# Slots of an expert-routed layer dealt four side by side to a partition, the slot table read in 4 KB rows, and early tile 5 turned ahead of the wait for that table

## The chip, the cores and the metric

The kernel runs on one core of one Trainium2 chip. TensorE (PE) multiplies; VectorE (DVE), ScalarE (ACT) and GpSimd (POOL) do the elementwise work; SyncE (SP) issues transfers; 16 DMA engines move the data. The time is device microseconds (us) of one launch. The median of three runs of the kernel before is 891.31 us, from 889.29 to 902.32.

## What is computed

```
y      = einsum('bct,bcd->bdt', x, cond_weights[itok])   # x: 64 x 64 x 1024 f32
logits = y @ W_gate + b_gate                             # 8 experts
top    = top_k(logits, 2)
out    = x + mean over the two chosen experts of relu(y @ W_e + b_e)
```

There are 64·64 = 4096 tokens of 1024 features. Each goes to two of eight experts, whose matrices are 1024 x 1024 in f32.

## The kernel before

**Token stage.** For 32 tiles of 128 tokens (n = 0 to 31) PE makes y (line 549), ACT copies it out (701) and writes it to `y_rows` in DRAM (704), and DVE turns it in 32 x 32 blocks (856) for the gate product (561). Every four tiles form a group g. For it DVE picks the top two experts (`choose`, 879) and works out each token's place in its expert's list (`slots`, 894). PE and DVE make the lists (`fill`, `list_out`), and SP writes them to `slot_table` in DRAM (`table_out`, 316). That table has 8 · 4096 words: for each expert the tokens it gets, in order, zero where none.

**Expert stage.** The table is cut into tiles of 128 slots. The rows of a tile are gathered from `y_rows` by four indirect transfers of 1 KB pieces, turned in 32 x 32 blocks by DVE, split into a high part `a_hi` (ACT) and a low part `a_lo` (DVE), and multiplied with the split weights in 48 matmuls (line 608). DVE adds the bias (`finish`, 987), ACT applies the relu and a factor of 0.5, and one indirect transfer adds the 128 result rows onto `out`, which holds a copy of x by then. An x copy is 14 transfers of 1 MB on SP's queue (`copy`, 337).

**Early tiles.** The first seven tiles (0 to 6) belong to expert 0 and run before the table is complete. `read_first(t)` (305, SP) fetches the 128 words of tile t: four transfers into `first`, a block of 32 partitions each, and one into `first_own`, one word to a partition. `read_from(t)` (970, DVE) makes the row numbers of the gather out of `first`; `early(t)` (442, POOL) issues the gather into `fetched[t % 2]`, which is named `raw` in the trace. `turn_early(t)` (1001, DVE) turns it into `early_t` (named `bias`), `early_hi(t)` (727, ACT) and `early_lo(t)` (1010, DVE) split it. `early_out` (976, DVE) makes the row numbers for the result of tiles 0 to 3 and then 4 to 6, out of `first_own`.

**The rest of the tiles.** When all eight groups are in the table, ACT issues its read, four transfers of 128 KB, one to each block of 32 partitions of `ys` (line 771, `slots_all`). DVE waits for it (1074), turns it (1076), multiplies it into `idx_all` (1078: row numbers of the gathers), and makes `idx_row` (1085 and `to_out`, 982: row numbers of the results). POOL's `gather` (458) of tile 7 waits for `idx_all`.

**Order.** Every engine runs the list that is written for it, in order. On DVE, `turn_early(5)` and `early_lo(5)` stand behind the wait for the table and the two steps on it; on ACT, `relu(3)` stands ahead of `early_hi(5)`. PE starts tile t when `a_lo` of it is there, and when the result of tile t-2 has been taken out of its half of PSUM (`s_bo`).

Of the kernel before, what the change touches and what calls it, by code (L numbers as in the profile page):

```python
# [7 lines left out]
P = 128  # L8
F32, F32R, BF16 = mybir.dt.float32, mybir.dt.float32r, mybir.dt.bfloat16
I32, U32, F16 = mybir.dt.int32, mybir.dt.uint32, mybir.dt.float16  # L10
ACTF = mybir.ActivationFunctionType
AX = mybir.AxisListType
# [15 lines left out]
def build(nc, x, itok, cond_w, gate_w, gate_b, exp_w, exp_b, out, y_dram, table):  # L28
    B, C, D = x.shape
    NCOND = cond_w.shape[0]  # L30
    E, _, H = exp_w.shape
    TOK = B * C
    PAIR = P // C
# [3 lines left out]
    G = 4  # L37
# [5 lines left out]
    EARLY = 7  # L43
# [5 lines left out]
    COLS = E * TPE  # L49
    Q = 4  # L50
    R = P // Q
# [13 lines left out]
    y_parts = y_dram.rearrange("n (q c) -> (n q) c", q=Q)  # L65


    slots_by = table.rearrange("(c a i) o -> i a (c o)", a=Q, i=R)
    slots_all = table.rearrange("(b i w) o -> i b (w o)", i=R, w=P)
    zeros_at = table.rearrange("(p c) o -> p (c o)", p=P)  # L70
    w_rows = exp_w.rearrange("e (k p) h -> (e k p) h", p=P)

    with ExitStack() as ctx:
        def sb(name, shape, dt=F32):
            return ctx.enter_context(nc.sbuf_tensor(name, shape, dt))
# [4 lines left out]
        def sem(name):  # L80
            return ctx.enter_context(nc.semaphore(name))
# [3 lines left out]
        with ExitStack() as lent:  # L85
            def lend(name, shape, dt=F32):
                return lent.enter_context(nc.sbuf_tensor(name, shape, dt))
# [4 lines left out]
        with ExitStack() as lent:  # L92
# [4 lines left out]
            ident = lend("ident", [P, P])  # L97
# [13 lines left out]
        ys = sb("ys", [P, G, D])  # L111
# [5 lines left out]
        idx_all = sb("idx_all", [P, Q, COLS], U32)  # L117
        idx_row = sb("idx_row", [P, COLS], U32)
        idx_g = sb("idx_g", [P, 2, Q], U32)
        idx_s = sb("idx_s", [P, OS], U32)  # L120
        first = sb("first", [P, EARLY, Q], U32)
        first_own = sb("first_own", [P, EARLY], U32)
        first_to = sb("first_to", [P, EARLY], U32)
        behind = sb("behind", [P, EARLY])
        part_q = sb("part_q", [P, 1])
# [96 lines left out]
        s_first = [sem(f"s_first{i}") for i in range(EARLY)]  # L222
        s_yx = [sem(f"s_yx{i}") for i in range(2)]
        s_from = sem("s_from")
        s_own = [sem(f"s_own{i}") for i in range(2)]
        s_run, s_fill2, s_list = sem("s_run"), sem("s_fill2"), sem("s_list")
        s_yg = [sem(f"s_yg{i}") for i in range(2)]
        s_cond, s_cw, s_cw2, s_gw, s_gr, s_gb = sem("s_cond"), sem("s_cw"), sem("s_cw2"), sem("s_gw"), sem("s_gr"), sem("s_gb")
# [40 lines left out]
        def tile(i, c):  # L269

            return i * 4 + c, i * 2 + c // 2, c % 4
# [22 lines left out]
        with nc.Block() as block:  # L294

            @block.sync
            def _(sp):
# [6 lines left out]

                def read_first(t):


                    sp.wait_ge(s_sc[t], LAND)
                    for q in range(Q):
                        sp.dma_start(first[q * R:(q + 1) * R, t, :], slots_by[:, :, t],  # L310
                                     allow_slow_non_contiguous=True).then_inc(s_first[t], 16)
                    sp.dma_start(first_own[:, t:t + 1], table[t * P:(t + 1) * P, :]).then_inc(s_own[t // G], 16)

                at = [sp.alloc_register(f"start{e}") for e in range(E)]

# [33 lines left out]
                for n in range(NTILE):  # L349
                    if n in STORES:  # L350
                        store(n)
                    elif n + X < NTILE:
                        sp.wait_ge(s_y, n + 1)
                        load(n + X)
                    if n in LIST:
                        table_out(LIST[n])
                    if n in READS:
                        read_first(READS[n])
# [6 lines left out]
                load_bias(0)  # L365
                table_out(NG - 3)
                read_first(4)
                copy(2)
                copy(3)
                table_out(NG - 2)  # L370
                read_first(5)
                copy(4)
                copy(5)
# [444 lines left out]
            def _(dve):  # L818
                own = Chain(dve, s_dve)
                V = nc.vector  # L820
# [14 lines left out]
                    own(V.tensor_tensor(stack[:, :], stack[:, :], ident[:, j * R:(j + 1) * R], ALU.add))  # L835
                own(V.tensor_copy(spread[:, :].rearrange("p (a i) -> p a i", a=Q), stack[:, :].unsqueeze(1).to_broadcast([P, Q, R])))
                dve.sem_inc(s_same, 1)
                dve.wait_ge(s_const, 2)
                own(V.tensor_copy(counts[:, :], count_i))
                own(V.tensor_copy(counts_h[:, :], counts[:, :]))  # L840
# [134 lines left out]

                def early_out(lo, hi):

                    dve.wait_ge(s_own[lo // G], (hi - lo) * 16)
                    to_out(first_to[:, lo:hi], first_own[:, lo:hi], behind[:, lo:hi])
                    dve.sem_inc(s_to, hi - lo)  # L980

                def to_out(to, src, empty):

                    own(V.tensor_scalar(empty, src, 1.0, empty_to[:, :], ALU.is_lt, ALU.mult))
                    own(V.scalar_tensor_tensor(to, src, -1.0, empty, ALU.add, ALU.add))

                def finish(t, e):
                    n, half, m = t
                    dve.wait_ge(s_bias, e * 16 + 16)
                    dve.wait_ge(s_mm, n + 1)  # L990
                    V.tensor_tensor(out_of(t), psO[m % 2][:, :], bias[:, bass.ds((e % 2) * H, H)], ALU.add).then_inc(s_bo, 1)  # L991

                def finish_early(t):

                    if t < FIRST:
                        dve.wait_ge(s_xout[t + 1], 16)
                    elif t % OS >= 2:
                        dve.wait_ge(s_yout[t % OS], 16 * NG)
                    finish(tile(0, t), 0)

                def turn_early(t):
                    dve.wait_ge(s_yx[t % 2], (t // 2 + 1) * (Q * 16))
                    if t:
                        dve.wait_ge(s_alo, t)
                    else:
                        dve.wait_ge(s_split, KD)
                    V.transpose(early_t.rearrange("p (k a i) -> p k a i", k=KD, a=Q),  # L1007
                                fetched[t % 2].rearrange("p (a k j) -> p k a j", k=KD, a=Q)).then_inc(s_zt, 1)

                def early_lo(t):  # L1010
                    dve.wait_ge(s_ahi, t + 1)
                    V.tensor_tensor(a_lo[:, t % 2, :], early_t, a_hi[:, t % 2, :], ALU.subtract).then_inc(s_alo, 1)  # L1012
# [18 lines left out]
                for n in range(NTILE):  # L1031
# [15 lines left out]
                    if n == NTILE - 4:  # L1047
# [12 lines left out]
                list_out(NG - 1)  # L1060
                finish_early(1)
                early_out(0, 4)
                read_from(5)
                turn_early(3)
# [4 lines left out]
                read_from(6)  # L1069
                schedule()  # L1070
                early_out(4, EARLY)
                finish_early(3)

                dve.wait_ge(s_tab, Q * 16)
                dve.wait_ge(s_yout[1], 16 * NG)
                own(V.transpose(ys[:, 1, :].bitcast(U32).rearrange("p (a b i) -> p b a i", a=Q, i=R),
                                ys[:, 0, :].bitcast(U32).rearrange("p (b a j) -> p b a j", a=Q, j=R)))
                own(V.tensor_scalar(idx_all[:, :, :].rearrange("p a c -> p (a c)"), ys[:, 1, :].bitcast(U32), float(Q),
                                    part_q[:, :], ALU.mult, ALU.add))
                dve.sem_inc(s_idx, 1)  # L1080
                turn_early(5)
                early_lo(5)
                for q in range(Q):
                    at = slice(q * R, (q + 1) * R)
                    own(V.tensor_copy(ys[at, 0, 0:COLS], ys[at, 1, q * COLS:(q + 1) * COLS].bitcast(U32)))
                to_out(idx_row[:, :], ys[:, 0, 0:COLS], ys[:, 0, COLS:2 * COLS])
                dve.sem_inc(s_idx, 1)
                finish_early(4)
                turn_early(6)
# [84 lines left out]
```

## Time and profile before

| | |
|---|---|
| median of three runs | 891.31 us (889.29 to 902.32) |
| the profiled execution | 889.16 us, of it a span of 887.5 us, mean granted TensorE clock 0.989 |
| PE busy | 848.7 us, 96% of the span |
| DVE, ACT, POOL busy | 425.3, 257.5, 451.4 us |
| DMA | 162.47 MB in 55,626 packets, 15,290 of them under 512 B |

The span is the part that the trace covers; 889.16 - 887.5 = 1.66 us lie around it. Busy time is a sum over the span; where it says nothing of what waits for what, the views of waits and the chain that ended last do.

### The profile page before, as it was taken

The page shows a single profiled execution, that of the slowest core. Times are in us where ns is not written, and L with a number is a line of the kernel's source. Part 1 is how long each engine was busy: PE and PEld are TensorE (multiplying, and loading weights), DVE is VectorE, ACT ScalarE, POOL GpSimd, SP SyncE. Part 2 cuts the span into 40 slices and gives each one's busy share as a digit, 9 for nine tenths or more (in the row PEclk, how much of TensorE's full clock was granted, in tenths as well). Part 3 has the DMA queues.
Part 4 walks back from the last instruction along what each step waited for, and adds up shares of the span by engine and source line. Part 5 has one row for each costly group of instructions (what it writes and reads, how often), then busy time and mean ns, then how long its engine had stood idle before and what let it go on. Part 6 is the DMA issues. An engine that isn't in the chain of part 4 may idle for free.

```text
span 887.5 us, 16689 instructions
## 1 busy us (share of the span) xinstructions
PE 848.7 (96%) x4154; PEld 672.3 (76%) x4155; DVE 425.3 (48%) x570; ACT 257.5 (29%) x310; POOL 451.4 (51%) x500
## 2 busy tenths in 40 slices
PE   8788799999999999999999999999999999999993
PEld 4444368788888888888888888888888888888882
DVE  5688886557643373335533373336433733333320
ACT  5655412133522251114211331115111511111220
POOL 3002224366467777654665556555755565554411
PEclk9899999999999999999999999999999999999997
DMA  9999698998965496446754494547664655444432
GB/s 338 418 398 361 225 308 291 340 339 256 269 153 121 100 305 132 106 95 198 197 103 92 98 294 104 108 100 212 170 118 95 189 115 108 90 101 90 89 48 47
DMA packets 55626, 162.47 MB, mean 183 GB/s; under 512 B 15290, under 2 KB 16378, under 8 KB 55578
## 3 DMA queue, kind: packets, MB, share of 16 engines
q0 software_dynamic: 24544, 76.74, 39.3%
q1 hardware_dynamic: 24314, 67.79, 21.4%
q10 hardware_dynamic: 6736, 17.57, 5.1%
q8 instruction: 14, 0.23, 0.1%
q14 instruction: 18, 0.15, 0.0%
HBM read 106.74 MB, written 70.52 MB: 200 GB/s over the span
## 4 chain that ended last, share of the span: by engine, by line
PE 83%; DVE 7%; DMA 5%; issue 2%; ACT 1%; ACTq 0%; POOL 0%; DVEq 0%; POOLq 0%
PE psO L608 82%; DMA y_rows<-ys 2%; DVE turned L856 2%; DMA ys<-slot_table 2%; DMA raw<-in_L_cond_weights 1%; DVE w_lo L869 1%; DVE place_hot L911 0%; DVE run_hot L919 0%; ACT ys L701 0%; ACT a_hi L731 0%; DVE bias L1007 0%; PE psG L561 0%; DVE idx_all L885 0%; DVE idx_all L884 0%; DVE idx_all L887 0%
## 5 line engine op out<-in xcount | busy, mean ns | idle before, releaser
L608 PE MATMUL psO<-w_hi,a_hi 128*128 (+1 forms) x1104 | 341.1, 390 | 1.4 <-DVE a_lo L1012 1.4
L608 PE MATMUL psO<-w_lo,a_hi 128*128 (+1 forms) x1104 | 339.9, 389 | 0.0
L608 PE MATMUL psO<-w_hi,a_lo 128*128 (+1 forms) x1104 | 339.9, 389 | 0.0
L466 POOL DMA_INDIRECT rows<-y_rows,idx_g x248 | 260.0, 1048 | 106.8 <-issue 54.0
L608 PEld LDWEIGHTS psO<-w_hi,a_hi 128*128 128x128 f32 x1104 | 206.4, 188 | 45.2 <-DVE a_lo L1012 1.8
L608 PEld LDWEIGHTS psO<-w_lo,a_hi 128*128 128x128 f32 x1104 | 207.2, 188 | 43.1
L608 PEld LDWEIGHTS psO<-w_hi,a_lo 128*128 128x128 f32 x1104 | 207.2, 188 | 43.1
L1029 DVE TENSOR_TENSOR a_lo<-ys,a_hi 128x1024 fp32r<-128x1024 f32 x62 | 76.0, 1225 | 113.9 <-ACT a_hi L737 75.3
L725 ACT ACTIVATE ys<-ys 128x1024 f32<-128x1024 f32 x33 | 35.1, 1062 | 259.8 <-DVE ys L991 210.9
L725 ACT ACTIVATE rows<-rows 128x1024 f32<-128x1024 f32 x33 | 35.0, 1062 | 247.6 <-DVE rows L991 218.1
L991 DVE TENSOR_TENSOR ys<-psO,bias 128x1024 f32<-128x1024 f32 x33 | 40.4, 1224 | 125.6 <-PE psO L608 92.9
L991 DVE TENSOR_TENSOR rows<-psO,bias 128x1024 f32<-128x1024 f32 x33 | 40.4, 1224 | 116.6 <-PE psO L608 81.7
L876 DVE TENSOR_TENSOR w_lo<-raw,w_hi 128x1024 f32 x56 | 65.3, 1223 | 35.7 <-ACT w_hi L720 17.9
L1018 DVE STREAM_TRANSPOSE ys<-rows 128x1024 f32<-128x1024 f32 x62 | 76.8, 1238 | 11.4 <-DMA rows<-y_rows,idx_g 11.4
L495 POOL DMA_INDIRECT out<-rows,idx_s x31 | 54.3, 1752 | 41.4 <-issue 19.3
L495 POOL DMA_INDIRECT out<-ys,idx_s x31 | 53.4, 1723 | 37.0 <-POOL idx_s L491 17.4
L462 POOL COPY idx_g<-idx_all 128x4 uint32 x62 | 27.5, 444 | 87.6 <-issue 54.2
L737 ACT CAST a_hi<-ys 128x1024 fp32r<-128x1024 f32 x62 | 65.1, 1050 | 10.1 <-issue 10.0
L452 POOL DMA_INDIRECT raw<-y_rows,from_q x28 | 29.9, 1068 | 66.2 <-DVE bias L1007 36.2
L720 ACT CAST w_hi<-raw 128x1024 f32 x56 | 55.4, 1050 | 6.6 <-DMA raw<-in_L_ffn_W_e 5.1
L856 DVE STREAM_TRANSPOSE turned<-ys 128x1024 f32<-128x1024 f32 x32 | 39.4, 1240 | 13.6 <-ACT ys L701 11.5
L701 ACT COPY ys<-psO 128x1024 f32<-128x1024 f32 x32 | 32.4, 1013 | 24.3 <-PE psO L549 17.2
(136 smaller groups left out, 331.7 us busy)
## 6 DMA issues: line engine op xcount, KB each, us to landing
raw<-in_L_ffn_W_e SPq DMA_DIRECT2D x56, 512.0 KB
y_rows<-ys ACTq DMA_DIRECT2D x32, 512.0 KB, 8.0
out<-in_x SPq DMA_DIRECT2D x14, 1024.0 KB
rows<-in_x SPq DMA_DIRECT2D x16, 512.0 KB, 11.0
more_x<-in_x SPq DMA_DIRECT2D x16, 512.0 KB, 10.6
bias<-in_L_ffn_b_e SPq DMA_DIRECT2D x8, 512.0 KB
rows<-y_rows,idx_g POOLq DMA_INDIRECT x248
raw<-in_L_ffn_W_e POOLq DMA_DIRECT2D x4, 512.0 KB, 8.9
```

Source lines behind the costliest of these rows:

```text
L466: pool.indirect_dma_start(out=rows[:, slot, a * DQ:(a + 1) * DQ], out_offset=None, in_=y_parts[0:(1 + TOK) * Q, :], in_offset=bass.Indirec ...
L495: pool.indirect_dma_start(out=out, out_offset=bass.IndirectOffsetOnAxis(ap=idx_s[:, m:m + 1], axis=0), in_=o_sb[m], in_offset=None, comput ...
L608: last = nc.tensor.matmul(ps[:, h * BANK:(h + 1) * BANK], a[:, p, k * P:(k + 1) * P], w[:, bass.ds(slot + (k * H + h * BANK), BANK)], star ...
L701: nc.scalar.copy(ys[:, s, :].rearrange("p (q k j) -> p q k j", q=Q, k=KD), psO[n % 2][:, :].rearrange("p (k q j) -> p q k j", q=Q, k=KD)). ...
L720: nc.scalar.copy(w_hi[:, bass.ds(at, H)], raw[:, k, :]).then_inc(s_hi, 1)
L725: nc.scalar.activation(out_of(t), out_of(t), ACTF.Relu, scale=0.5).then_inc(s_out, 1)
L737: nc.scalar.copy(a_hi[:, m % 2, :], ys[:, m % 2, :]).then_inc(s_ahi, 1)
L856: V.transpose(turned[:, g % 2, :, s * R:(s + 1) * R], ys[:, s, :].rearrange("p (b i) -> p b i", i=R)).then_inc(s_turn, 1)
L876: V.tensor_tensor(w_lo[:, bass.ds(at, H)], raw[:, k, :], w_hi[:, bass.ds(at, H)], ALU.subtract).then_inc(s_split, 1)
L991: V.tensor_tensor(out_of(t), psO[m % 2][:, :], bias[:, bass.ds((e % 2) * H, H)], ALU.add).then_inc(s_bo, 1)
L1018: V.transpose(ys[:, p, :].rearrange("p (k a i) -> p k a i", k=KD, a=Q), rows[:, p, :].rearrange("p (a k j) -> p k a j", k=KD, a=Q)).then_i ...
L1029: V.tensor_tensor(a_lo[:, p, :], ys[:, p, :], a_hi[:, p, :], ALU.subtract).then_inc(s_alo, 1)
```

## The change

Tile t of the table holds the words 128t to 128t+127. Before, word 32a + i of it went to partition i of each block of 32, column a, and the gather number a fetched into column block a; so partition p of the tile was slot p. Now word 4i + a goes there, so partition 32a + i is slot 4i + a.

1. `first` is read in runs of four words (16 bytes) to a partition, not in four single words. The transfer into `first_own` and its semaphore are gone: five transfers of SP to a tile become four.
2. `early_out` gets its column out of `first` on DVE: a cast, a multiplication with a 0/1 mask `quarter` (one reduction at the start of the kernel makes it), and a reduction over the four.
3. The whole table is read in one row of 4 KB to a partition, not in eight of 512 bytes. DVE needs one more step on it, a rearranging copy ahead of the turn; the next steps read in a rearranged order.
4. `turn_early(5)` and `early_lo(5)` now stand ahead of the wait for the table.

```diff
-    slots_by = table.rearrange("(c a i) o -> i a (c o)", a=Q, i=R)
-    slots_all = table.rearrange("(b i w) o -> i b (w o)", i=R, w=P)
+    slots_by = table.rearrange("(c i a) o -> i c (a o)", a=Q, i=R)
+    slots_all = table.rearrange("(i b w) o -> i b (w o)", i=R, w=P)
...
                     for q in range(Q):
-                        sp.dma_start(first[q * R:(q + 1) * R, t, :], slots_by[:, :, t],
-                                     allow_slow_non_contiguous=True).then_inc(s_first[t], 16)
-                    sp.dma_start(first_own[:, t:t + 1], table[t * P:(t + 1) * P, :]).then_inc(s_own[t // G], 16)
+                        sp.dma_start(first[q * R:(q + 1) * R, t, :], slots_by[:, t, :]).then_inc(s_first[t], 16)
...
+                own(V.tensor_reduce(quarter[:, :], ident[:, :].rearrange("p (a i) -> p a i", a=Q), AX.X, ALU.add))
...
                 def early_out(lo, hi):
 
-                    dve.wait_ge(s_own[lo // G], (hi - lo) * 16)
-                    to_out(first_to[:, lo:hi], first_own[:, lo:hi], behind[:, lo:hi])
+                    some = parted[:, 0:hi - lo, :]
+                    own(V.tensor_copy(some, first[:, lo:hi, :]))
+                    own(V.tensor_tensor(some, some, quarter[:, :].unsqueeze(1).to_broadcast([P, hi - lo, Q]), ALU.mult))
+                    own(V.tensor_reduce(first_f[:, lo:hi], some, AX.X, ALU.add))
+                    to_out(first_to[:, lo:hi], first_f[:, lo:hi], behind[:, lo:hi])
                     dve.sem_inc(s_to, hi - lo)
...
                 finish_early(3)
+                turn_early(5)
+                early_lo(5)
 
                 dve.wait_ge(s_tab, Q * 16)
                 dve.wait_ge(s_yout[1], 16 * NG)
-                own(V.transpose(ys[:, 1, :].bitcast(U32).rearrange("p (a b i) -> p b a i", a=Q, i=R),
-                                ys[:, 0, :].bitcast(U32).rearrange("p (b a j) -> p b a j", a=Q, j=R)))
-                own(V.tensor_scalar(idx_all[:, :, :].rearrange("p a c -> p (a c)"), ys[:, 1, :].bitcast(U32), float(Q),
+                table_at = [ys[:, i, :].bitcast(U32) for i in range(2)]
+                own(V.tensor_copy(table_at[1].rearrange("p (b a j) -> p b a j", a=Q, j=R),
+                                  table_at[0].rearrange("p (b j a) -> p b a j", a=Q, j=R)))
+                own(V.transpose(table_at[0].rearrange("p (a b i) -> p b a i", a=Q, i=R),
+                                table_at[1].rearrange("p (b a j) -> p b a j", a=Q, j=R)))
+                own(V.tensor_scalar(idx_all[:, :, :].rearrange("p a (i b) -> p a i b", i=R),
+                                    table_at[0].rearrange("p (a b i) -> p a i b", a=Q, i=R), float(Q),
                                     part_q[:, :], ALU.mult, ALU.add))
                 dve.sem_inc(s_idx, 1)
-                turn_early(5)
-                early_lo(5)
                 for q in range(Q):
                     at = slice(q * R, (q + 1) * R)
-                    own(V.tensor_copy(ys[at, 0, 0:COLS], ys[at, 1, q * COLS:(q + 1) * COLS].bitcast(U32)))
-                to_out(idx_row[:, :], ys[:, 0, 0:COLS], ys[:, 0, COLS:2 * COLS])
+                    own(V.tensor_copy(ys[at, 1, 0:COLS].rearrange("p (i b) -> p i b", i=R),
+                                      ys[at, 0, q * COLS:(q + 1) * COLS].bitcast(U32).rearrange("p (b i) -> p i b", i=R)))
+                to_out(idx_row[:, :], ys[:, 1, 0:COLS], ys[:, 1, COLS:2 * COLS])
                 dve.sem_inc(s_idx, 1)
```

On DVE, behind `finish_early(3)` (the row `ys<-psO,bias`), where the table is taken in (`bias<-raw` turns an early tile, `a_lo<-bias,a_hi` splits it). Before:

```order
L991 TENSOR_TENSOR ys<-psO,bias 128x1024
L1076 STREAM_TRANSPOSE ys<-ys 128x8x4x32
L1078 TENSOR_SCALAR idx_all<-ys,part_q 128x1024
L1007 STREAM_TRANSPOSE bias<-raw 128x1024
L1012 TENSOR_TENSOR a_lo<-bias,a_hi 128x1024
L1085 CAST ys<-ys 32x256 x4
L984 TENSOR_SCALAR ys<-ys,empty_to 128x256
L985 SCALAR_TENSOR_TENSOR idx_row<-ys 128x256
L991 TENSOR_TENSOR rows<-psO,bias 128x1024
L1007 STREAM_TRANSPOSE bias<-raw 128x1024
```

The same place on DVE in the changed kernel, whose lines have other numbers:

```order
L993 TENSOR_TENSOR ys<-psO,bias 128x1024
L1009 STREAM_TRANSPOSE bias<-raw 128x1024
L1014 TENSOR_TENSOR a_lo<-bias,a_hi 128x1024
L1081 COPY ys<-ys 128x1024
L1083 STREAM_TRANSPOSE ys<-ys 128x8x4x32
L1085 TENSOR_SCALAR idx_all<-ys,part_q 128x1024
L1091 CAST ys<-ys 32x256 x4
L986 TENSOR_SCALAR ys<-ys,empty_to 128x256
L987 SCALAR_TENSOR_TENSOR idx_row<-ys 128x256
L993 TENSOR_TENSOR rows<-psO,bias 128x1024
L1009 STREAM_TRANSPOSE bias<-raw 128x1024
```

The turn and the low part of tile 5 moved up over the table's turn and `idx_all`, and a copy came in ahead of the table's turn.

Also on DVE, `early_out(0, 4)` between the end of tile 1 (`more_x<-psO,bias`) and the turn of tile 3. Before:

```order
L991 TENSOR_TENSOR more_x<-psO,bias 128x1024
L984 TENSOR_SCALAR behind<-first_own,empty_to 128x4
L985 SCALAR_TENSOR_TENSOR first_to<-first_own,behind 128x4
L973 TENSOR_SCALAR from_q<-first,part_q 128x4
L1007 STREAM_TRANSPOSE bias<-raw 128x1024
```

The same place in the changed kernel:

```order
L993 TENSOR_TENSOR more_x<-psO,bias 128x1024
L978 CAST parted<-first 128x16
L979 TENSOR_TENSOR parted<-parted,quarter 128x16
L980 TENSOR_REDUCE first_f<-parted 128x4
L986 TENSOR_SCALAR behind<-first_f,empty_to 128x4
L987 SCALAR_TENSOR_TENSOR first_to<-first_f,behind 128x4
L972 TENSOR_SCALAR from_q<-first,part_q 128x4
L1009 STREAM_TRANSPOSE bias<-raw 128x1024
```

Three small steps came in ahead of the row numbers; the same three, on three columns, stand ahead of `finish_early(3)` for tiles 4 to 6.

## Rows read from the trace of the kernel before

**Rows 1.** The page: chain that ended last, share of the span by line.
```profile
PE psO L608 82%; DMA y_rows<-ys 2%; DVE turned L856 2%; DMA ys<-slot_table 2%; DMA raw<-in_L_cond_weights 1%; DVE w_lo L869 1%; DVE place_hot L911 0%; DVE run_hot L919 0%; ACT ys L701 0%; ACT a_hi L731 0%; DVE bias L1007 0%; PE psG L561 0%; DVE idx_all L885 0%; DVE idx_all L884 0%; DVE idx_all L887 0%
```
**Rows 2.** The waits of PE: for whom, us in total, times, longest.
```profile
PE psO L608 <- DVE a_lo L1012: 1.4, 1, 1.4
```
**Rows 3.** Busy time of each engine in stretches of the span.
```profile
core 0: us, PE busy (x) PEld busy (x) DVE busy (x) ACT busy (x) POOL busy (x), PEclk, DMA share, GB/s
...
60.00:80.00 20.00, 16.86 (x151) 8.55 (x150) 17.69 (x47) 11.76 (x23) 4.35 (x4) 1.00 1.01 369
...
154.00:176.00 22.00, 21.30 (x94) 17.29 (x93) 12.96 (x30) 3.87 (x4) 8.25 (x8) 1.00 1.03 342
...
400.00:874.00 474.00, 473.70 (x2089) 391.75 (x2087) 188.74 (x160) 118.78 (x117) 260.14 (x288) 1.00 0.55 128
```
**Rows 4.** The chain in order of time: start, duration, what.
```profile
156.70 14.11 DMA ys<-slot_table
170.84 1.26 DVE ys L1076
172.12 0.76 DVE idx_all L1078
173.08 1.26 DVE bias L1007
174.36 1.06 ACT a_hi L731
175.44 1.24 DVE a_lo L1012
176.72 697.00 PE psO L608 x3072
873.99 1.24 DVE rows L991
```
**Rows 5.** PE in order of time, two matmuls a row: start, duration, what, idle before.
```profile
174.68 0.61 PE L608 MATMUL psO<-w_hi,a_lo 128*128 128x512 f32 x2
176.72 0.74 PE L608 MATMUL psO<-w_hi,a_hi 128*128 128x512 f32 x2 [1.42 <-DVE a_lo L1012]
177.30 0.63 PE L608 MATMUL psO<-w_lo,a_hi 128*128 128x512 f32 x2
```
**Rows 6.** DVE in order of time.
```profile
143.94 0.22 DVE L984 TENSOR_SCALAR behind<-first_own,empty_to 128x4 f32<-128x4 uint32 x1
...
150.67 1.25 DVE L1007 STREAM_TRANSPOSE bias<-raw 128x1024 f32<-128x1024 f32 x1 [2.06 <-DMA raw<-y_rows,from_q]
...
162.62 0.16 DVE L985 SCALAR_TENSOR_TENSOR first_to<-first_own,behind 128x3 uint32<-128x3 uint32 x1
164.56 1.23 DVE L991 TENSOR_TENSOR ys<-psO,bias 128x1024 f32<-128x1024 f32 x1 [1.77 <-PE psO L608]
...
176.59 1.35 DVE L1085 CAST ys<-ys 32x256 f32<-32x256 uint32 x4
...
179.00 1.23 DVE L991 TENSOR_TENSOR rows<-psO,bias 128x1024 f32<-128x1024 f32 x1 [0.21 <-DVE idx_row L985]
...
182.50 1.23 DVE L1012 TENSOR_TENSOR a_lo<-bias,a_hi 128x1024 fp32r<-128x1024 f32 x1 [1.12 <-ACT a_hi L731]
```
**Rows 7.** ACT in order of time.
```profile
165.82 1.06 ACT L725 ACTIVATE ys<-ys 128x1024 f32<-128x1024 f32 x1 [9.82 <-DVE ys L991]
```
**Rows 8.** POOL in order of time (its indirect transfers, from issue's start to its end).
```profile
143.85 0.94 POOL L452 DMA_INDIRECT raw<-y_rows,from_q  x1 [0.30 <-issue]
...
151.04 0.94 POOL L452 DMA_INDIRECT raw<-y_rows,from_q  x1 [0.30 <-issue]
...
179.07 0.95 POOL L466 DMA_INDIRECT rows<-y_rows,idx_g  x1 [0.30 <-issue]
...
220.35 1.61 POOL L483 DMA_INDIRECT out<-ys,first_to  x1 [0.30 <-issue]
229.20 1.01 POOL L491 COPY idx_s<-idx_row 128x1 uint32 x1 [7.24 <-DMA out<-ys,first_to]
```
**Rows 9.** The page: DMA queue, packets, MB, share of 16 engines' span.
```profile
q1 hardware_dynamic: 24314, 67.79, 21.4%
```

More of the change, by code:

```diff
@@ L121, in build @@
         first = sb("first", [P, EARLY, Q], U32)
-        first_own = sb("first_own", [P, EARLY], U32)
+        first_f = sb("first_f", [P, EARLY])
+        parted = sb("parted", [P, Q, Q])
+        quarter = sb("quarter", [P, Q])
         first_to = sb("first_to", [P, EARLY], U32)
@@ L224, in build @@
         s_from = sem("s_from")
-        s_own = [sem(f"s_own{i}") for i in range(2)]
         s_run, s_fill2, s_list = sem("s_run"), sem("s_fill2"), sem("s_list")
```

## Prediction

> **What bounds the kernel now.** I read the chain that ended last first [rows 1]: 82% of the span is one line, PE's expert products (L608). In order of time [rows 4] it is one unbroken piece of 3072 matmuls, 697.00 us from 176.72 on. That is 64 tiles of 48 matmuls, so 697.00 / 64 = 10.89 us a tile. The stretches say the same: from 400 to 874 us PE is busy 473.70 of 474.00 us at full granted clock [rows 3]. Nothing that the other engines do there is worth time unless it makes PE wait.
>
> Next, PE's waits. In the expert stage PE waits once: 1.4 us for `a_lo` of line 1012 [rows 2]. It is the start of early tile 5, at 176.72 [rows 5]. The chain just ahead of it names the cause [rows 4]: the table's read lands at 156.70 + 14.11 = 170.81; DVE turns it (1.26), makes `idx_all` (0.76), and only then turns tile 5 (173.08), ACT splits it (174.36), DVE finishes it (175.44 + 1.24 = 176.68). Tile 5 needs nothing of the table. It only stands behind it in DVE's list.
>
> The token stage, up to about 115 us, is another matter. There DVE is busy 17.69 of 20 us [rows 3]; the chain's larger pieces in it are `turned` (L856) and DVE's small steps [rows 1]. DMA is saturated too (share 1.01), but the only transfers of tokens in the chain, `y_rows<-ys` with 2%, lie in the first 38 us, ahead of the first list.
>
> **The change part by part.**
>
> *Tile 5 ahead of the wait.* Two matmuls start every 10.89 / 24 = 0.454 us, so after the last pair of tile 4 at 174.68 tile 5 could start at 175.13. It started at 176.72: 1.59 us lost. Its first pair then took 0.58 to the next (177.30 - 176.72) in place of 0.454, another 0.13 [rows 5]. At stake are 1.72 us, and no more.
>
> When is tile 5 ready now? Its gather's last issue is at 151.04 [rows 8]. For tile 4 the last issue was at 143.85 and the wait for it ended at 150.67 [rows 8, 6], 6.82 later; so tile 5's rows are in at 157.9, even with the delay below at 158.6. DVE ends `finish_early(3)` at 164.56 + 1.23 = 165.79 [rows 6], turns tile 5 by 167.05 (1.26), ACT is then through with its relu (165.82 + 1.06 = 166.88 [rows 7]), and the split takes what it took before: from the turn's start to the end of `a_lo` 176.68 - 173.08 = 3.60 us [rows 4]. So `a_lo` is ready at 165.8 + 3.6 = 169.4, 5.7 us ahead of 175.13. The 1.72 us go whole.
>
> *Does a second wait take its place?* The next that depends on the table is tile 6, which DVE turns behind `idx_row` and `finish_early(4)`. I start from the old landing, 170.84. DVE is free at 169.4, so it is there. The new copy (128 x 1024, one source) is not in the trace. Its lower bound is 0.76, the one-source step on as many words (L1078), its upper one 1.24, the two-source step (L1012) [rows 4]. I take 1.24, for the rearranged order, and raise `idx_all` to 1.24 too. Then `idx_all` is complete at 170.84 + 1.24 + 1.26 + 1.24 + 0.06 for the joints = 174.64, before at 172.88: 1.76 later. Then, as before, from L1085's start to the start of `finish_early(4)` 179.00 - 176.59 = 2.41, and from there to the end of `a_lo` of tile 6 182.50 + 1.23 - 179.00 = 4.73 [rows 6]: 174.64 + 0.1 + 2.41 + 4.73 = 181.9. PE needs it at 175.13 + 10.89 = 186.0. Spare: 4.1 us (before 176.72 + 10.89 - 183.73 = 3.9). So PE doesn't wait here until the table lands 4.1 us later than it did.
>
> The Trainium skill, "VectorE: DVE Perf Modes" (What auto-detection actually checks), has a single-source op between SBUF tensors use both read ports if the outermost dimensions are even, whatever the steps; by that both the copy and `idx_all` would stay at 0.76, the estimate of the spare would be 5.1 us, and the time the same.
>
> *Tile 7* is gathered by `idx_all`. Its last issue was at 179.07 [rows 8], now 1.76 later at 180.8, and with tile 4's 6.82 it lands at 187.7. DVE gets to it only after `finish_early(5)`, which waits for PE's end of tile 5, 186.0, and ends at 187.4. From there turn, high and low part take some 3.8 (3.60 and joints): 191.5, needed at 186.0 + 10.9 = 196.9. Spare 5.4 us.
>
> *`early_out`.* Three steps more, twice. I price them by 0.22 for a small step (143.94) [rows 6], 0.25 with its joint: 0.75 us each time. The first moves tile 3's turn, its `a_lo`, POOL's first result transfer and the issue of tile 5's gather by 0.75. Tile 4's turn, behind them, waits 2.06 us for its gather anyway (150.67), and that gather is issued before. The second falls into the 1.77 us in which DVE waits for PE at 164.56 [rows 6]. Both cost nothing on the path; were that cover gone, it would be 1.5 us. `quarter` is one small step ahead of 11 us, where DVE waits for the first y.
>
> *`read_first`.* Of five transfers a tile four remain, and their pieces go from 4·128 + 128 = 640 of 4 bytes to 128 of 16 bytes: 7 · 512 = 3584 packets fewer. A packet of that queue took on average 0.214 · 16 · 887.5 / 24314 = 0.125 us [rows 9], which is mostly of large ones; so 3584 are worth 0 to 448 us of one DMA engine, 0 to 28 of all sixteen, over some 90 us. Nobody on the path waits for a transfer of that stretch, so I put it at 0. Work that it could shorten: the x copies and the table's read, whose 14.11 us [rows 4] stand in a stretch with DMA share 1.03 [rows 3]. Its rows of 4 KB in place of eight of 512 bytes go the same way. A sooner landing brings nothing: DVE is at the table at 169.4.
>
> *Sum.* 889.16 (profiled execution, 887.5 and 1.66 around it) - 1.72 = 887.4. The tail behind the last matmul (873.99 on [rows 4]) is untouched. The median of the runs shown lies 2.15 above the profiled execution. One of the three is far off; the mean of the other two, 890.30, lies 1.1 above. I add that 1.1: **888.5 us** for the median of new runs. About 2%, 18 us, is what a measurement of this kernel can tell from no change, so this is within it by far.
>
> **The rivals.**
>
> A. *The next wait takes it back.* The table lands more than 4.1 us later, and tile 6 takes tile 5's place as the one that PE waits for. For it: DMA is full in that stretch [rows 3], and POOL's gathers, which now come 0.75 later, and the x copies share it. A partition's row now is one 4 KB piece, so the load on a single DMA engine is no better spread. Against it: fewer packets in all. At 6 us later PE loses 1.9: 887.4 + 1.9 + 1.1 = 890.4. The Trainium skill, "DMA: Bandwidth & Descriptors" (Specifications), puts line rate at pieces of 512 B and more; by it the old read was at line rate already and the 16-byte pieces of `first` are still below, so neither gets faster and the landing stays at 170.8; that leaves the time at 888.5 and the spare at 4.1.
>
> B. *The token stage gets shorter.* If DMA was what DVE and PE in truth waited for there, 3584 fewer packets would show. DVE's idle time is the ceiling: 2.3 us in 20 [rows 3], so some 6 from 60 to 115 us. Half of it would give 885.5. Against it: the chain holds no transfer there.
>
> C. *The new dealing slows the indirect transfers, and the kernel gets slower.* A result tile's 128 rows of 4 KB now go to rows of `out` in an order that jumps by four slots between partitions; so do the gathers. Result transfers run one at a time. One was issued at 220.35 and waited out until 229.20 [rows 8]: 8.85 us. The limit is PE's 10.89 a tile. It decides from 2.0 us more per transfer. At 4 us more, 62 tiles would lose 2.0 each, less the 3 buffers of slack: some 115 us, 1000 us. Against it: number and size of pieces are the same, and with DMA share 0.55 [rows 3] there is room.
>
> D. *Nothing moves*, because tile 5 is held by something else, or run to run noise of the token stage (its waits are short and many) covers 1.7 us: 890.3.
>
> **How the numbers follow.** Forecast, tile 5's wait gone and no new one: 0.70. A: 0.08. B: 0.08. C: 0.02. D: 0.12. Low end: B with half its ceiling, 885.5. High end: A's 890.4 and, since the three runs shown spread by 2 us without the far one, as much on top: 892.5. Faster by over 2% would need 18 us; even B's whole ceiling doesn't reach that: 0.01. Slower by over 2% is C or a disturbed median: 0.03. Within: 0.96.
>
> **What would show each step.** Right: PE without a wait in the expert stage, its piece of the chain starting with or before tile 0 and running over tile 5's start; the end of `a_lo` for tile 5 near 169.4; DVE's wait ahead of the table under 1.5 us in place of 5; the last matmul ends near 872. The copy's duration tells between 0.76 and 1.24. Wrong: a wait of PE for `a_lo` at tile 6 (A); tile 0 starting a microsecond or more away from 115 us (B, D); POOL waiting for result transfers by more than 8.85 us after their issue, with PE waiting for PSUM (C).

## The result, and the profile after

The changed kernel takes 889.12 us, the median of 16 executions, from 886.35 to 891.52. The kernel before, run beside it 16 times, has a median of 895.31, from 889.29 to 902.32. The ratio of the two is 0.9931, with a 95% interval of 0.9906 to 0.9955: 6.2 us less, well under 2% and clear of no change. The time lies 0.6 us from the forecast 888.5. The gain doesn't fit as well: 1.7 us were forecast, 6.2 measured (4.0 to 8.4 by the interval). The median of three runs, 891.31, from which the forecast started, was 4 us under that of 16. The spread tells more than the medians: 8 of the 16 executions of before took 895 us or more, and none of the changed kernel more than 891.52.

The profiled executions are almost equal: 889.16 before, 888.81 after. PE in the changed kernel, whole span: who it waited for, us, times, longest (the four longest and the only one at the expert products):

```profile
PE psG L559 <- DVE turned L855: 5.7, 5, 1.1
PE psR L579 <- ACT LT L708: 5.1, 4, 4.2
PE psO L635 <- POOLq L414: 2.8, 1, 2.8
PE psL L571 <- DVEq L921: 2.7, 2, 2.0
...
PE psO L606 <- issue: 0.3, 1, 0.3
```

The row of [rows 2] is gone. What is left at the products is 0.28 us in another place. The chain of the changed kernel between 140 and 215 us:

```profile
142.07 66.86 PE psO L606 x294
208.93 0.28 issue
209.21 5.96 PE psO L606 x25
```

294 matmuls from the end of tile 1 to the end of tile 7 run without a break, over the place of the wait in [rows 4, 5]. DVE in the same profile:

```profile
145.13 0.18 DVE L979 TENSOR_TENSOR parted<-parted,quarter 128x16 f32<-128x16 f32 x1
...
165.56 1.22 DVE L993 TENSOR_TENSOR ys<-psO,bias 128x1024 f32<-128x1024 f32 x1 [1.16 <-PE psO L606]
166.70 1.23 DVE L1009 STREAM_TRANSPOSE bias<-raw 128x1024 f32<-128x1024 f32 x1
169.04 1.23 DVE L1014 TENSOR_TENSOR a_lo<-bias,a_hi 128x1024 fp32r<-128x1024 f32 x1 [1.11 <-ACT a_hi L729]
170.19 1.08 DVE L1081 COPY ys<-ys 128x1024 uint32<-128x1024 uint32 x1
171.30 1.25 DVE L1083 STREAM_TRANSPOSE ys<-ys 128x1024 uint32<-128x1024 uint32 x1
172.59 1.28 DVE L1085 TENSOR_SCALAR idx_all<-ys,part_q 128x1024 uint32<-128x1024 uint32 x1
...
180.28 1.26 DVE L1014 TENSOR_TENSOR a_lo<-bias,a_hi 128x1024 fp32r<-128x1024 f32 x1 [1.12 <-ACT a_hi L729]
```

Tile 5 is ready at 170.27, and DVE goes on to the table without any wait (5.05 us before). Two profiles that differ by 0.4 us of span can't show a gain of 6.2: the rest of it has to come from executions that these two profiles don't show.

### The profile page after: what moved, and what is told of

Same layout as the page of the kernel before. It is cut to its first block, busy times and chain, and to the rows that moved or that the text cites. A ratio compares the mean times of both kernels' runs of the same rounds, so it can differ in the third digit from the quotient of the medians.

```text
span 887.1 us, 16691 instructions
## 1 busy us (share of the span) xinstructions
PE 851.0 (96%) x4154; PEld 674.1 (76%) x4155; DVE 428.5 (48%) x578; ACT 256.9 (29%) x310; POOL 446.5 (50%) x500
## 4 chain that ended last, share of the span: by engine, by line
PE 88%; DVE 6%; DMA 2%; issue 2%; ACT 1%; ACTq 0%; POOL 0%; DVEq 0%; POOLq 0%
PE psO L606 85%; DVE turned L855 2%; PE psO L547 2%; DMA y_rows<-ys 1%; ACT ys L699 1%; DMA raw<-in_L_cond_weights 1%; DVE w_lo L868 1%; PE psG L559 0%; DVE run_hot L918 0%; DVE place_hot L910 0%; DVE idx_all L884 0%; DVE idx_all L883 0%; DVE idx_all L886 0%; DVE raw L885 0%; PE psL L571 0%
## 5 line engine op out<-in xcount | busy, mean ns | idle before, releaser
L464 POOL DMA_INDIRECT rows<-y_rows,idx_g x248 | 255.7, 1031 | 106.8 <-issue 52.1
L855 DVE STREAM_TRANSPOSE turned<-ys 128x1024 f32<-128x1024 f32 x32 | 39.4, 1239 | 13.4 <-ACT ys L699 11.1
```

Of the source, the lines that this page charges most:

```text
L464: pool.indirect_dma_start(out=rows[:, slot, a * DQ:(a + 1) * DQ], out_offset=None, in_=y_parts[0:(1 + TOK) * Q, :], in_offset=bass.Indirec ...
L855: V.transpose(turned[:, g % 2, :, s * R:(s + 1) * R], ys[:, s, :].rearrange("p (b i) -> p b i", i=R)).then_inc(s_turn, 1)
```

## Experiments

T is the moved tile 5, F the other reading of `first` (with `early_out`), R the table's rows of 4 KB, S the new dealing of tiles 7 and up with DVE's rearranging copy. The changed kernel is T+F+R+S. The runs below came in three sets, each with its own executions of before, and these differ: the medians are 895.35, 891.53 and 892.17, and 19 of 35, 7 of 35 and 7 of 17 executions took 895 us or more. The kernels that have no such long executions stay at 888.6 to 889.7 in all three sets. So what a change gains over before depends on the set, and neither a median nor a ratio carries over from one set to another without loss.

**First set: the parts.** `tile5_only` is T:

```diff
                 finish_early(3)
+                turn_early(5)
+                early_lo(5)
...
                 dve.sem_inc(s_idx, 1)
-                turn_early(5)
-                early_lo(5)
```

> The kernel before with tile 5's turn and low part moved ahead of the wait for the table, and nothing else. Theory W (the table's read lands late by a varying amount, and before each us of it went straight into PE's wait for tile 5; moving tile 5 ahead buys slack of 4 to 5 us): takes the whole difference of the changed kernel, 5 to 6 us off the median and most of the spread. Theory P (fewer 4-byte packets in the token stage make the difference, the moved tile only the 1.7 us of the trace): 1.5 to 2 us off the median, the spread stays. The profile: no wait of PE for tile 5, a_lo of it near 169.4 us.

Measured: 891.19 (889.94 to 897.01), ratio 0.9959 (0.9929 to 0.9990). So T alone gives 3.7 us by the ratio and 4.2 by the medians, with an interval of 0.9 to 6.4 us. That is nearer to theory W than to P, though the 1.7 of the trace isn't excluded by this run alone. The spread shows it better: one of its 12 executions took 895 us or more. In its profile PE has no wait for tile 5, whose `a_lo` is there at 172.3 and not near 169.4, since `finish_early(3)` began at 167.58, 3.0 us later than in [rows 6]. But it waits 1.4 us elsewhere (below).

`tile5_back` is F+R+S, the changed kernel with `turn_early(5)` and `early_lo(5)` put back behind `idx_all`.

> The changed kernel with tile 5's turn and low part put back behind idx_all. Theory W: nearly all of the gain is gone, within 1 us of the kernel before or slower, since the copy and the slower idx_all (2.6 us by the trace after: 1.08 and 1.28 in place of 0.75, less what the landing gains) now stand ahead of tile 5; PE's wait for tile 5 is 2 to 4 us where the table lands at 170.8. Theory P: 3 to 5 us faster than before still, less the wait for tile 5.

Measured: 888.57 (886.87 to 891.09), ratio 0.9922 (0.9889 to 0.9955). This expectation fell in both its forms. With F, R and S in it the kernel is as fast without T as with it. DVE in its profile:

```profile
167.32 1.08 DVE L1079 COPY ys<-ys 128x1024 uint32<-128x1024 uint32 x1 [0.60 <-DMA ys<-slot_table]
168.44 1.25 DVE L1081 STREAM_TRANSPOSE ys<-ys 128x1024 uint32<-128x1024 uint32 x1
```

DVE gets the table at 167.3, with 0.6 us of waiting; before it was 170.8 [rows 4]. Its PE doesn't wait for tile 5 at all. So in this kernel the earlier landing cures the same wait that T cures by moving the tile. It doesn't follow that the new read of the table does so by itself: `rows_only`, below, has it and gains nothing.

`first_only` is F:

```diff
-                        sp.dma_start(first[q * R:(q + 1) * R, t, :], slots_by[:, :, t],
...
-                    sp.dma_start(first_own[:, t:t + 1], table[t * P:(t + 1) * P, :]).then_inc(s_own[t // G], 16)
+                        sp.dma_start(first[q * R:(q + 1) * R, t, :], slots_by[:, t, :]).then_inc(s_first[t], 16)
```

> The kernel before with only the reading of the early tiles' slots changed: runs of 16 bytes in place of single words, no transfer into first_own, three more small steps in early_out. Theory W: no change of the median within 1 us. Theory P: 3 to 5 us faster, and a narrower spread.

Measured: 899.19 (889.92 to 903.15), ratio 1.0032 (0.9989 to 1.0075). The packets (P) alone are refuted as the source of the gain. Its median is 3.8 us over that of before, more than the 1 us that W allowed, but the interval of the ratio includes no change. The profile, at 896.6 us, shows what the single profile of before hides. Its chain, and PE two matmuls a row behind the wait:

```profile
156.59 17.40 DMA ys<-slot_table
```

```profile
179.89 1.22 PE L607 MATMUL psO<-w_hi,a_hi 128*128 128x512 f32 x2 [5.03 <-DVE a_lo L1015]
180.91 1.05 PE L607 MATMUL psO<-w_lo,a_hi 128*128 128x512 f32 x2
181.77 1.05 PE L607 MATMUL psO<-w_hi,a_lo 128*128 128x512 f32 x2
...
185.18 0.62 PE L607 MATMUL psO<-w_hi,a_hi 128*128 128x512 f32 x2
185.63 0.62 PE L607 MATMUL psO<-w_lo,a_hi 128*128 128x512 f32 x2
```

```profile
180.00:185.00 5.00, 5.00 (x12) 3.94 (x13) 4.16 (x8) 1.48 (x2) 3.61 (x5) 0.50 0.99 324
```

The table lands at 174.0, 3.2 us later than in [rows 4], and PE waits 5.0 us in place of 1.4. Behind that wait the granted clock is 0.50, the lower of the two levels: a pair starts every 0.85 us in place of 0.45, until 185. That makes 185.18 - 179.89 = 5.29 us for six pairs that would take 2.85 at full clock: some 2.5 us more. Behind the wait of 1.42 in [rows 5] the clock stayed at full.

`rows_only` is R, with the slots dealt as before:

```diff
-    slots_all = table.rearrange("(b i w) o -> i b (w o)", i=R, w=P)
+    slots_all = table.rearrange("(i b w) o -> i b (w o)", i=R, w=P)
```

> The kernel before with only the table's read changed to rows of 4 KB to a partition; the slots stay dealt as before, so no rearranging copy is needed, idx_all is read in another order. Theory W: the table may land sooner, idx_all takes 1.28 in place of 0.75; PE's wait for tile 5 changes by 0.5 us up, less what the landing gains: within 1 us of before if the landing stays at 14 us, up to 4 us faster if it lands 4 us sooner. Theory P: within 1 us.

Measured: 894.4 (890.27 to 899.34), ratio 0.9997 (0.9960 to 1.0035). DVE takes up the table at 167.50 in its profile and doesn't wait for it, so it landed at least 3.3 us sooner than in [rows 4]. For that theory W allowed up to 4 us less than before; the ratio shows no gain, so theory W didn't foresee this kernel.

```profile
167.50 1.25 DVE L1076 STREAM_TRANSPOSE ys<-ys 128x1024 uint32<-128x1024 uint32 x1
```

In the same profile, at 890.27, tile 5's wait is gone, but PE waits 1.3 us at 209.6 to 210.9. The chain ahead of that:

```profile
152.84 15.92 DMA out<-in_x
168.78 8.02 DMA out<-in_x
176.82 7.09 DMA out<-in_x
185.97 1.32 SPq L335
188.02 14.36 DMA raw<-in_L_ffn_W_e
210.87 663.99 PE psO L608 x2928
```

A second thing is late here: the weights of expert 1, which SP loads behind the x copies. ACT and DVE split them ahead of the first tile of that expert (tile 8), so its `a_lo` comes late. The chain of `tile5_only` reads the same (16.30 us for the weights from 187.55, PE on from 212.34). SP's last eight copies start at 152.2 and 153.4 in these two, which have five transfers to a tile in `read_first`, and at 150.4 and 150.1 in the changed kernel and `tile5_back`, which have four, where PE waits 0.3 us and nothing. Before itself starts them at 150.75, so these few don't show that F brings the copies forward. All traces together speak for it (those of `copies_held` aside): the six traces with five transfers start them at 150.8 to 153.4, 152.1 on average, the seven traces with four at 148.7 to 151.3, 150.0 on average. That this shortens the wait at tile 8 isn't shown: `first_and_tile5`, which has F, waits 1.5 us there.

**Second set: is it the dealing, and how much spare is there?** `first_and_rows` is F+R, that is `tile5_back` without S and without the copy on DVE.

> The kernel before with both read changes together (early slots in runs of 16 bytes and no first_own; the table in rows of 4 KB), tile 5 left behind the table, and the slots of the other tiles dealt as before, so that there is no rearranging copy. Against tile5_back only the new dealing of tiles 7 and up and its copy on DVE are missing. Theory L (two late landings make the difference: the table's, which the rows bring forward by 3.5 us, and those of expert 1's weights behind the x copies, which one SP transfer fewer per tile brings forward by 1 to 3 us): within 1.5 us of tile5_back's 888.6, with its narrow spread. Theory S (the new dealing of the main tiles makes the gathers and result transfers easier): like rows_only, 893 to 895.

Measured: 889.44 (887.78 to 892.9), ratio 0.9971 (0.9948 to 0.9993) to a before of 891.53. The median is within 1 us of that of `tile5_back`, as L has it. By the ratios the two differ (0.9971 and 0.9922), but it is before that moved between the sets, by 3.8 us; no set has both kernels. DVE turns the table at 165.73, without a copy, and no execution took over 892.9. So the gain doesn't need the new dealing of the main tiles; a share of it below 1 us isn't excluded.

`before_late4`, `after_late4` and `after_late8` put copies on ACT ahead of the issue of the table's read:

```diff
                 act.wait_ge(s_turn, NTILE)
+                for i in range(4):
+                    nc.scalar.copy(rows[:, 0, :], rows[:, 1, :]).then_inc(s_late, 1)
+                    act.wait_ge(s_late, i + 1)
```

> The kernel before with four copies of 128 x 1024 on ACT ahead of the issue of the table's read, which delay it by 4.4 us; they write to a buffer that nothing reads again. Theory L with the clock: PE's wait for tile 5 grows by 4.4 us to some 6, the granted clock falls to half for some 5 us behind it, which costs another 2.5 (first_only: six pairs of 0.85 us in place of 0.45 behind a wait of 5.0): 889.2 + 6.9 = 896 for an execution like the profiled one, the median 899 to 901. Without the part of the clock: 893.6.

Measured: 892.39 (889.57 to 903.19), ratio 1.0026 (0.9984 to 1.0068). The expectation fell. In its profile ACT issues the read from 161.84 on, 6.5 us later than before, and DVE gets it at 171.44, 0.6 later than before. The chain:

```profile
163.44 7.98 DMA ys<-slot_table
177.34 696.63 PE psO L609 x3072
```

The read took 8.0 us where it took 14.1. In this pair of profiles the later issue hardly moved the landing. It isn't so in general: in `after_late8` below, with rows of 4 KB, the read is issued 9.2 us later than in the changed kernel, and the table comes 6.0 us later or more. 4 of the 10 executions of `before_late4` took 898 us or more, against 7 of 35 over 895 of before; what those did isn't traced.

> The changed kernel with the same delay of 4.4 us ahead of the table's read. By the spare of the prediction (4.1 us counted from 170.8, and the rows land some 3.5 us before that): nothing, within 1 us of 889.1, no wait of PE at tile 6. If the slack behind the table is used up otherwise: 2 to 4 us slower.

Measured: 889.75 (887.78 to 895.74), ratio 0.9979 (0.9947 to 1.0012). No wait at tile 6, and the median 0.6 off. But 3 of the 10 executions took 895.05 to 895.74, which no other kernel with T and R did. Its profile, at 890.15, has two waits with 2.0 us in all at later tiles, at 209.8 and 254.5 us. What the three met isn't known.

> The changed kernel with eight such copies, 8.9 us. The table then lands at about 176; from DVE's copy to the end of a_lo of tile 6 the trace after has 11.35 us, so it would be ready at 187.4 against PE's need at 187.0: PE waits 0 to 1 us at tile 6, 889 to 891. This finds the end of the spare. If the spare were the 4.1 us of the prediction alone, PE would wait 4 us and more with the clock halved behind it: 895 and up.

Measured: 889.71 (887.73 to 890.6), ratio 0.9957 (0.9926 to 0.9989). DVE, and the chain:

```profile
176.15 1.08 DVE L1085 COPY ys<-ys 128x1024 uint32<-128x1024 uint32 x1 [5.37 <-DMA ys<-slot_table]
```

```profile
142.03 45.10 PE psO L607 x198
187.54 686.08 PE psO L607 x3024
```

DVE starts on the table at 176.15 in place of 170.19, 6.0 us later, and PE stands still from 187.13 to 187.54, at the start of tile 6. So the spare is 5.6 us, counted from DVE's own arrival at 170.19. The expectation (0 to 1 us of waiting, 889 to 891) held.

**Third set: where does the late landing come from, and what do the long executions show?** `copies_held`:

```diff
+                sp.wait_ge(s_tab, Q * 16)
                 for c in range(6, len(left)):
                     copy(c)
```

> The kernel before, with the last eight x copies held on SP until the table's read has landed. Theory L says that the table's read takes 14 us and more because it shares the DMA engines with the x copies in pieces eight times smaller: then it lands some 3 us after its issue, at about 160, tile 5 is turned in time and PE doesn't wait for it. The copies then end some 8 us later (at about 197 in place of 189), and with them the loads of expert 1's weights: PE waits 5 to 10 us at the first tile of expert 1, some 895 in all. If the landing is slow for another reason, it stays near 170.

Measured: 903.97 (903.61 to 904.49 in four executions), ratio 1.0116 (1.0064 to 1.0169). The table lands at 164.42, where the held copies start, so its read took some 6 us from its last issue and not the 3 that were expected. The chain:

```profile
164.42 8.31 DMA out<-in_x
...
183.79 9.48 DMA out<-in_x
196.44 15.35 DMA raw<-in_L_ffn_W_e
220.26 13.70 PE psO L609 x48
```

PE doesn't wait for tile 5. It waits 10.8 us for expert 1's weights, and the tile behind takes 13.70 us in place of 10.89, again at a clock of 0.50. 10.8 + 2.8 + 0.6 of a later wait, less the 1.7 for tile 5, plus 1.6 for a slower tile 0 (see below) and 0.2 for its later start, make 14.3 of the 14.4 by which the span is longer. The 895 of the expectation left out the clock, and the wait came out over its range. With the copies held, the read was 8 us shorter than in [rows 4]. That the copies beside it are what made it long is likely by this; how much they cost isn't fixed, since in `before_late4` the read took 8.0 us beside them. The spread of the four executions is 0.9 us (before in the same set: 889.70 to 899.85 in 16 of 17, the last at 903.79); the wait for the weights would hide a smaller one at tile 5.

`first_and_tile5` is F+T.

> first_only (median 899.2, and a wait of 5.0 us for tile 5 in its profile) with tile 5 moved ahead of the wait for the table. Theory L: tile 5's wait and the halved clock behind it made first_only slow, so this falls to 889 to 891 with few executions over 895, though the table's read still lands at 171 to 174. If the 16-byte reads are slow for another reason, it stays near 899.

Measured: 889.47 (887.0 to 892.16), ratio 0.9948 (0.9922 to 0.9975). F alone was 899.19, ratio 1.0032. The two moved steps of DVE take off 7.5 us by the ratios (0.9948 / 1.0032) and 9.7 by the medians, which are of different sets, and none of the 12 executions took over 892.16, where 10 of the 12 of `first_only` took over 895. In the profile DVE takes up the table at 171.16 without a wait, so when it landed isn't seen. So tile 5's place behind the table is what made `first_only` slow, to within the 1 us or so that the sets leave open.

`before_look1` and `before_look2` are the kernel before, unchanged, for two more traces.

> The kernel before, unchanged, for one more trace. If it is one of the executions at 889 to 892: PE's wait for tile 5 at most 2 us, granted clock full behind it. If it is one at 895 to 902: a wait of 4 us or more for tile 5, half clock for some 5 us behind it, or waits for expert 1's weights at 210 to 240 us.

> The kernel before, unchanged, for a second further trace, with the same two expectations: a short wait for tile 5 at full clock if it comes out at 889 to 892, and a wait of 4 us or more with the clock halved behind it, or waits for expert 1's weights, if it comes out at 895 to 902.

The first took 899.79 us, the second 890.23. Chain of the first:

```profile
157.14 20.71 DMA ys<-slot_table
177.88 1.26 DVE ys L1076
180.13 1.26 DVE bias L1007
182.48 1.24 DVE a_lo L1012
183.76 35.22 PE psO L608 x144
...
242.18 642.22 PE psO L608 x2832
```

The waits of its PE at the products, and two stretches (us, PE busy, PEld, DVE, ACT, POOL, clock, DMA, GB/s):

```profile
PE psO L608 <- DVE a_lo L1012: 8.1, 1, 8.1
...
PE psO L608 <- DVE a_lo L1029: 1.2, 1, 1.2
```

```profile
180.00:185.00 5.00, 1.24 (x3) 1.04 (x4) 3.63 (x6) 1.04 (x1) 2.54 (x4) 0.50 0.99 358
185.00:190.00 5.00, 5.00 (x15) 3.88 (x15) 3.62 (x5) 2.11 (x2) 3.60 (x5) 0.64 0.50 161
```

The same code, the same wait as in [rows 2, 4]: the table lands at 177.85 in place of 170.81, and PE waits 8.1 us in place of 1.4. The sum against [rows 4]: 6.7 for the wait, 35.22 - 3 · 10.89 = 2.5 for the halved clock, 1.2 for a wait at tile 10, together 10.4, of a span longer by 10.6. The second trace reads:

```profile
115.77 5.90 PE psO L608 x18
158.67 12.54 DMA ys<-slot_table
```

Its table lands at 171.2, 0.4 later than in [rows 4], and yet PE waits under 0.5 us for tile 5, since PE itself comes later: its first 18 matmuls took 5.90 us in place of 4.30. So the wait has two ends that move, and the landing moves by more. Both traces came out as their expectations had it.

## Why the prediction was right, and where it was not

*Tile 5's wait goes whole, and no new one comes.* Right. Tile 5 was ready 170.27 - 165.56 = 4.71 us after `finish_early(3)` began (forecast 169.4 - 164.56 = 4.8).

*"At stake are 1.72 us, and no more."* This term was mis-sized, and it is the step of the prediction that failed. 1.72 is right for the profiled execution alone, which is near the short end of what before does. The wait grows with the lateness of the table, and this moves: it landed at 170.8 and 177.9 in two traces of before, with waits of 1.4 and 8.1 us, and at 174.0 in `first_only`, with 5.0. Behind the waits of 5.0 and 8.1 us the halved clock adds some 2.5. So the term is 1.7 in one execution of before and 10.6 in another. That the mean over the executions makes the 6.2 us fits this, but only three traces of before exist, so the mean itself isn't measured. It is no fixed number either: in the second and third set, where before had fewer long executions, the kernels without them (`first_and_rows`, `first_and_tile5`) gained 2.6 and 4.6 us by their ratios.

*The sum.* That 888.5 came so near to 889.12 is in part luck. It started from a short execution, where before and after are closest. The 1.1 that it added for new runs came from two executions of before; it was right for the changed kernel, and 4 us short of the median that before then had.

*The two single profiles.* They differ by 0.4 us of span, not 1.7. Tile 0's first 18 matmuls took 5.86 us in place of 4.30, at a granted clock of 0.67 between 115 and 120 us (before 1.00). The stretch in before, then in the changed kernel:

```profile
115.00:120.00 5.00, 5.00 (x35) 3.96 (x35) 4.19 (x17) 0.00 (x0) 0.00 (x0) 1.00 1.03 391
115.00:120.00 5.00, 5.00 (x16) 4.02 (x16) 4.25 (x15) 0.00 (x0) 0.00 (x0) 0.67 1.03 382
```

The second further trace of the unchanged kernel has 5.90 for them, so this belongs to the execution and not to the change. -1.72 + 1.56 - 0.29 (PE began tile 0 at 115.03, not 115.32) + 0.28 = -0.17; the last matmul ended 0.22 earlier.

*The table's read: "a sooner landing brings nothing."* Right with T in place: `tile5_back` and the changed kernel are within 0.6 us. Without T it matters, but only together with F: `tile5_back` and `first_and_rows` have no long executions, `rows_only` has six of twelve. The Trainium skill, "DMA: Bandwidth & Descriptors" (Specifications), puts line rate at pieces of 512 B and more, and rival A said by it that the landing would stay at 170.8. For this read the runs disagree: in rows of 4 KB the table was with DVE at 167.3 (`tile5_back`), 165.7 (`first_and_rows`) and by 167.5 (`rows_only`), in rows of 512 bytes at 170.8 to 177.9 in the three traces of before, beside the same copies; the measurement decides. How each would do alone on the DMA engines no run here shows.

*DVE's prices.* The copy took 1.08, between the bounds 0.76 and 1.24. `idx_all` took 1.28, just over its upper bound, the four casts 1.67 in place of 1.35. The rule weighed there, from "VectorE: DVE Perf Modes" (What auto-detection actually checks) of the Trainium skill, by which both table steps would stay at 0.76, isn't borne out: 1.08 and 1.28. `early_out`'s three steps took 0.61 us (144.93 to 145.54), forecast 0.75, and were hidden as said.

*The spare ahead of tile 6.* Forecast 4.1 us from 170.84, so up to 174.9; `after_late8` puts it at 5.6 us from 170.19, so up to 175.7. The order of things was right. The end lies 0.8 us later than forecast, since PE itself reached tile 6 at 187.1 and not 186.0, and the steps from the copy to `a_lo` take 11.35 us and not 11.1.

*Rival A* didn't come. *Rival B* (a shorter token stage) neither: tile 0 begins 0.3 us earlier in the profile after. *Rival C* fell: with and without the new dealing 888.57 and 889.44. *Rival D* is true of the two profiled executions, and not of the medians.

*What was missing.* The forecast put no price on the weights of expert 1. They stand behind the same copies, and PE waited 1.3, 1.4 and 1.5 us at tile 8 in `rows_only`, `tile5_only` and `first_and_tile5`, and 10.8 in `copies_held`. In the changed kernel it is 0.3.

**Open.** `rows_only` has six of twelve executions between 895.58 and 899.34, though its profile (890.27) shows no wait for tile 5. Whether the table came late in those or the weights did isn't traced. So it is open too why F, which alone gains nothing, makes the long executions go once R is there (`rows_only` 0.9997, `tile5_back` 0.9922 in one set). What sets a landing of 171 against one of 178 wasn't followed either.

## What to carry to other kernels

A wait that ends with a transfer in a crowded stretch is not one number. Its trace shows one draw, and what removing it is worth has to be asked of many; the spread of the timed runs, 889 to 902 here, was the sign of it in plain sight. It also follows that the gain is a statement on this spread: with few long executions in before it is smaller. Take work that needs nothing of the transfer out from behind it in program order, and count PE's wait with the clock behind it: 1.4 us cost 1.7, 8.1 us cost over 10.

## What the runs showed of the hardware that I had not expected

- PE's granted clock fell to 0.50 behind waits of 5.0, 8.1 and 10.8 us at the expert products and stayed there for some 5 us, at 2.4 to 2.8 us of cost (`first_only`, `before_look1`, `copies_held`); behind a wait of 1.4 us it stayed at full (before).
- In one pair of profiles (before, `before_late4`) a read issued 6.5 us later landed 0.6 us later: 8.0 us in flight in place of 14.1.
- The same read, of 512 KB in pieces of 512 bytes, was in flight for 12.5, 14.1 and 20.7 us in three executions of one kernel (before and its two further traces).
- Reordering what a DVE step reads, at the same number of elements, took a one-source step on 128 x 1024 words (`idx_all`) from 0.75 to 1.28 us.
